# A Mamba-2 mixer: z of all four chunks at once, step widths one slot sooner, statistics of the first norm in other slots

## The reference, cut to what matters

```python
zxbcdt = x @ in_proj_w.T
z, xBC, dt = jnp.split(zxbcdt, [D_INNER, D_INNER + CONV_DIM], axis=-1)
dt = jax.nn.softplus(dt + dt_bias)
xBC = silu(causal_conv(xBC, conv_w) + conv_b)      # 4 taps, per channel
xs, Bm, Cm = jnp.split(xBC, [D_INNER, D_INNER + D_STATE], axis=-1)
dA = jnp.exp(dt * -jnp.exp(A_log))
# scan over tokens: h = h * dA_t + dt_t * x_t (outer) B_t;  y_t = h . C_t
y = (y + D * xs) * silu(z)
y = y * rsqrt(mean(y * y) + eps) * norm_w
return y @ out_proj_w.T
```

## Time and profile before

| what | value |
|---|---|
| median of 3 runs | 643.15 us (638.3 to 648.62) |
| profiled execution, time | 639.96 us |
| profiled execution, span | 638.0 us |
| mean granted TensorE clock | 0.929 |
| TensorE busy | 546.5 us, 86% |
| VectorE busy | 444.5 us, 70% |
| ScalarE busy | 360.4 us, 56% |
| GpSimd busy | 267.7 us, 42% |

### The profile page before, as it was taken

The page is one execution under the profiler, slowest core; times in us unless marked ns, Lnnn a source line. Parts: engine busy times, 40 slices in busy tenths (PEclk is TensorE's granted clock), DMA queues, the critical chain, the costliest instruction groups (busy, mean ns, idle before and its releaser), DMA issues.

```text
span 638.0 us, 13876 instructions
## 1 busy us (share of the span) xinstructions
PE 546.5 (86%) x3457; PEld 452.1 (71%) x3457; DVE 444.5 (70%) x1657; ACT 360.4 (56%) x1013; POOL 267.7 (42%) x324
## 2 busy tenths in 40 slices
PE   5588888898998989978789999973599999999593
PEld 3467677776777877766467877763599999999441
DVE  3746868577776657768568999997366666666267
ACT  4767584848485674834446656641266556666234
POOL 2213323241314123322102666677266666676333
PEclk9889999889998789989989999995699999999797
DMA  9399999990000000000064111111222222222383
GB/s 271 115 256 172 182 179 186 172 188 19 0 18 1 2 17 2 17 1 17 18 173 142 44 36 44 40 39 56 56 66 72 66 74 69 69 69 65 111 210 100
DMA packets 76395, 54.78 MB, mean 86 GB/s; under 512 B 10524, under 2 KB 69408, under 8 KB 76184
## 3 DMA queue, kind: packets, MB, share of 16 engines
q1 hardware_dynamic: 70352, 43.39, 33.9%
q0 software_dynamic: 4320, 8.99, 4.2%
q10 hardware_dynamic: 1640, 1.45, 0.7%
HBM read 40.62 MB, written 31.58 MB: 113 GB/s over the span
## 4 chain that ended last, share of the span: by engine, by line
PE 40%; issue 34%; DVE 11%; POOL 10%; DMA 4%; ACT 1%; ACTq 1%; POOLq 0%; SPq 0%; DVEq 0%
PE bank L1852 11%; PE bank L1870 10%; PE bank L1722 3%; PE bank L1738 3%; POOL arena L279 2%; PE bank L1728 2%; POOL arena L291 1%; POOL queue L1277 1%; DMA arena<-in_conv_w 1%; PE bank L1843 1%; POOL arena L267 1%; POOL x L297 1%; PE bank L1713 1%; POOL arena L294 1%; DVE nmx L1485 1%
## 5 line engine op out<-in xcount | busy, mean ns | idle before, releaser
L284 POOL TENSOR_TENSOR arena<-arena,half_neg 128x1 f32<-128x1 f32 x32 | 17.6, 550 | 196.0 <-ACT arena L442 196.0
L1317 POOL DMA_INDIRECT results<-arena x71 | 75.7, 1067 | 55.0 <-ACT arena L1416 50.4
L1852 PE MATMUL bank<-front,arena 128*128 128x128 f32 x568 | 78.5, 282 | 1.1 <-issue 0.3
L1870 PE MATMUL bank<-h_all,front 128*128 x568 | 75.5, 276 | 0.1
L1277 POOL DMA_INDIRECT queue<-arena,pos x64 | 63.1, 985 | 28.5 <-issue 13.8
L1852 PEld LDWEIGHTS bank<-front,arena 128*128 128x128 f32 x568 | 70.6, 195 | 4.3 <-issue 3.1
L1870 PEld LDWEIGHTS bank<-h_all,front 128*128 128x128 f32 x568 | 69.4, 193 | 0.3 <-issue 0.3
L1635 DVE COPY arena<-arena 128x516 f32 x71 | 35.9, 506 | 42.5 <-PE bank L1852 34.6
L684 PE MATMUL bank<-h_hi,wc_hi 128*128 128x512 f32 x96 | 46.6, 486 | 15.5 <-ACT arena L436 15.5
L1410 ACT ACTIVATE front<-bank 128x128 f32<-128x128 f32 x71 | 19.7, 278 | 53.6 <-PE bank L1843 52.7
L1648 DVE TENSOR_SCALAR front<-bank,arena 128x128 f32<-128x128 f32 x142 | 42.8, 342 | 4.7 <-PE bank L1852 4.5
(11 more groups left out here) (282 smaller groups left out, 1498.1 us busy)
## 6 DMA issues: line engine op xcount, KB each, us to landing
queue<-in_pad_rows SPq DMA_DIRECT2D x8, 2178.0 KB, 33.1
arena<-queue SPq DMA_DIRECT2D x71, 66.0 KB, 1.9
rows<-mod_rows SPq DMA_DIRECT2D x8, 384.0 KB, 6.3
x_keep<-x SPq DMA_DIRECT2D x8, 256.0 KB, 2.3
arena<-in_w SPq DMA_DIRECT2D x1, 2048.0 KB, 8.8
h_all<-in_w SPq DMA_DIRECT2D x1, 2048.0 KB, 8.6
h_all<-results SPq DMA_DIRECT2D x8, 256.0 KB, 4.8
arena<-results SPq DMA_DIRECT2D x8, 256.0 KB, 5.1
```

The source lines that it names most:

```text
L1317: pool.indirect_dma_start(k.results, bass.IndirectOffsetOnAxis(ap=xg[:, c, D:D + 1].bitcast(I32), axis=0), yw[:, c, :], None).then_inc(S[f ...
L1852: mm = t_.matmul(bank[(2 if g < NG // 2 else 6) + p][:, g * P:g * P + P], wc[:, p, g * P:g * P + P], xt[:, p, :], start=True, stop=True)
L1870: mm = t_.matmul(bank[4 + p][:, 0:D], ht[:, p, g * P:g * P + P], w2[:, e, g, :], start=(g == 0), stop=(g == NG - 1))
```

## The change

Four things.

1. TensorE computes all four z products of a slot c = 0 ahead of the chunk's product (L791 to L799), where two stood behind it. ScalarE evicts all four at the head of the slot.
2. silu(z) of the last chunk of a sequence gets three buffers instead of two, so that its eviction waits for the gating product of f - 3. The arena grows by 256 columns.
3. The step widths move from slot c = 1 into c = 0: DVE's first two operations behind L551, ScalarE's exp and ln behind its four copies and ahead of L414 and the flat eviction, DVE's last two into the end of the slot. ScalarE's exp(dt * A) and the silu table load move to the head of slot c = 1.
4. The first norm's statistics, for sequences 3 to 7, are taken in slots c = 0 (chunks 0 and 1) and c = 1 (chunks 2 and 3) instead of four in slot c = 2. In slot c = 0 they stand behind L593 and ahead of L607. The addition L639 moves with them to c = 1. POOL's root L304 stays in c = 2, L521 and L450 in c = 3.

```diff
-        zs = sb("zs", [P, 2, NC, DI]); xn1 = ...
+        zs = sb("zs", [P, 2, NC - 1, DI]); zs_last = sb("zs_last", [P, 3, DI]); xn1 = ...
+        def z_rows(f, i):
+            return zs[:, f % 2, i, :] if i + 1 < NC else zs_last[:, f % 3, :]
 # ScalarE, z_leaves
-                if f >= 2:
-                    wait(act, "s_yz", NC * (f - 2) + i + 1)
+                ago = 2 if i + 1 < NC else 3
+                if f >= ago:
+                    wait(act, "s_yz", NC * (f - ago) + i + 1)
 # ScalarE, body, head of the slot
                 if front and c == 0:
-                    z_leaves(f, 0)
-                    z_leaves(f, 1)
-                if front and c == 1:
-                    ... (wait d_neg; exp; wait d_exp; ln)
+                    for i in range(NC):
+                        z_leaves(f, i)
 ...
+                if front and c == 1:
+                    ... (wait d_dax; exp into da48; early silu)
 # ScalarE, body, behind the copies
                 if front and c == 0:
-                    z_leaves(f, 2)
-                    z_leaves(f, 3)
+                    ... (wait d_neg; exp; wait d_exp; ln)
                 ... (L414)
-                if front and c == 1:
-                    ... (wait d_dax; exp into da48; early silu)
                 if front and c == 0:
                     flat_leaves(f)
 # VectorE, body, behind L551
+                if front and c == 0:
+                    ... (L526, L537, which stood before and behind L534 for c == 1)
 ...
-                if gl < NB and c == 2:
+                norm = ({2: (0, 1, 2, 3)} if gl < 3 else {0: (0, 1), 1: (2, 3)}).get(c, ()) if gl < NB else ()
+                if norm:
                     wait(dve, "l1_ag", NC * gl)
-                    for i in range(NC):
+                    for i in norm:
                         v.bn_stats(st1[:, i, :], x[:, gl * NC + i, :]).then_inc(S["l1_st"], 1)
                 if chunk(s) and c == 0:
                     ... (L607)
 ...
-                if gl < NB and c == 2:
+                if norm and norm[-1] == NC - 1:
                     ... (L639)
-                if front and c == 1:
+                if front and c == 0:
                     ... (L643), and the same for L651
 # TensorE, body
                 if front and c == 0:
-                    z(f, 0)
-                    z(f, 1)
+                    for i in range(NC):
+                        z(f, i)
 ... (L791 to L799 of chunk s - 1)
-                    if front and c == 0:
-                        z(f, 2)
-                        z(f, 3)
```

More of the change, by code:

```diff
@@ L383, in body @@
                                   bias=mod[:, 0, 0, g:g + 1]).then_inc(S["f_ev"], 1)
+                if front and c == 1:
+                    wait(act, "d_dax", f + 1)
+                    act.wait_ge(S["set_pool"], 1)
+                    if f >= 1:
+                        wait(act, "o_w", seventh["da", f - 1] + 1)
+                    ac.activation(da48[:].rearrange("p (i w) -> p i w", i=3)[:, 0::2, :], dax[:].rearrange("p (o w) -> p o w", o=1).broadcast_to([P, 2, NC * NH]),
+                                  ACT.Exp).then_inc(S["d_da"], 1)
+                    ac.activation(early[:], ones[:, 0:1], ACT.Silu)
                 if between:
@@ L407, in body @@
                 if front and c == 0:
-                    z_leaves(f, 2)
-                    z_leaves(f, 3)
+                    if f == 0:
+                        act.wait_ge(S["w_in2"], 16 * 6)
+                        ac.activation(a_exp[:], a_log[:], ACT.Exp)
+                    wait(act, "d_neg", f + 1)
+                    ac.activation(dte[:], dtn[:], ACT.Exp).then_inc(S["d_exp"], 1)
+                    wait(act, "d_exp", f + 1)
+                    ac.activation(dtl[:], dte[:], ACT.Ln, bias=1.0).then_inc(S["d_ln"], 1)
                 if chunk(s) and c < 3:
@@ L552, in body @@
                                     bank[2][:, DI:DI + P].rearrange("p (o i) -> p o i", o=1).broadcast_to([P, NH, P]), ALU.mult).then_inc(S["s_mt"], 1)
+                if front and c == 0:
+                    wait(dve, "f_ev", ring["z", f, 3] + 1)
+                    wait(dve, "d_dt", f)
+                    v.tensor_tensor(dtw[:].rearrange("p (k h) -> p k h", h=NH), dtr[:].rearrange("p (k h) -> p k h", h=NH),
+                                    dt_b[:].rearrange("p (o h) -> p o h", o=1).broadcast_to([P, NC, NH]), ALU.add).then_inc(S["d_raw"], 1)
+                if front and c == 0:
+                    wait(dve, "d_raw", f + 1)
+                    v.scalar_tensor_tensor(out=dtn[:], in0=dtw[:], scalar=-1.0, in1=dtw[:], op0=ALU.mult, op1=ALU.min).then_inc(S["d_neg"], 1)
                 if front and c == 3:
@@ L626, in body @@
                         dve.nop(nofuse=True).then_inc(S["o_r"], 1)
-                if gl < NB and c == 2:
-                    wait(dve, "l1_st", NC * (gl + 1))
-                    for i in range(NC):
+                if norm:
+                    wait(dve, "l1_st", NC * gl + norm[-1] + 1)
+                    for i in norm:
                         v.bn_aggr(mv1[:, i, :], st1[:, i, :]).then_inc(S["l1_ag"], 1)
@@ L809, in body @@
                         t_.matmul(bank[4][:, 0:DI], b_rows[:, t % 2, :], xdw[:, t % 2, :], start=True, stop=True).then_inc(S["s_smm"], 1)
-                elif front and c == 0:
-                    z(f, 2)
-                    z(f, 3)
                 if front and c == 0:
@@ L1076, in after_mixer @@
             late[0] += n
-            assert late[0] <= 19568
+            assert late[0] <= 19824
             return k.carve(late[0] - n, shape)
```

27 lines of the change are left out of this document (6 added, 21 removed).

## The result

| what | before | after |
|---|---|---|
| median, first comparison | 644.9 us (638.3 to 648.6) | 655.9 us (654.2 to 659.2) |
| ratio to before, 95% interval | | 1.021 (1.015 to 1.027) |
| median, second comparison | 652.1 us | 661.1 us |
| ratio to before, 95% interval | | 1.015 (1.008 to 1.022) |
| profiled execution, time / span | 639.96 / 638.0 us | 659.21 / 657.2 us |

What follows compares the result with a forecast made beforehand. It took the mixer for a TensorE stream whose few stalls are paid in full, with half clock on top. -8.9 + 11.1 - 0.4 + 1.5 = +3.3 us on 639.96 gave 643.3, by the median 646.5; forecast 645, range 638 to 652.

Steps and rivals of the forecast that it cites:

- The trade: TensorE's 1.78 us stall in slots c = 2 goes, about 2.5 us at the out-projection of c = 0 comes; chance 0.55.
- c = 2, stall at the convolution gone: ScalarE no longer idles 1.78 us, so TensorE's wait for L436 goes in five slots c = 2: -8.9 us.
- c = 0, out-projection later: L607 and the out-projection come 2.03 us later in four slots, 1.60 and 1.4 in two: +11.1 us.
- c = 3: Slots c = 3 stay near 8.0 us, as L521 still waits for POOL's L304: -0.4 us over four.
- clock: New stall brings half clock in five of six slots c = 0 and 1; 7.4 + 5.6 against 11.5: +1.5 us.
- The stall for z(2)'s bank: In slot c = 0 TensorE waits 0.55 us until ScalarE has evicted z(0), whose bank z(2) writes.
- the two long slots: Two slots c = 0 with two smaller stalls each, at half clock before; their 5.6 us was taken to stay.
- Rival B: Slower: clock stays low for longer, six slots c = 0 pay 2.8 us each; +12.7, 653 to 656 us; chance 0.2.
- Rival A: Faster: the new stall at the out-projection does not come, L607 having slack; -15.2, 625 to 628 us; chance 0.13.
- Rival C: ScalarE is not freed, its exp waiting for DVE's negated widths; +8, 648 to 651 us; chance 0.1.
- The term for c = 0: Two of the four statistics in DVE's run before L607 delay the out-projection by 0.43 us in four sequences.
- a cover of 5 us: If POOL's L291 holds the moved L639 in c = 1, about 5 us of DVE idle before L548 hides it.

Runs made afterwards that it cites:

- The second pair: Kernel after and kernel before profiled once more without an edit; after 661.11 us for 652.1 before, ratio 1.015.
- e9_filler: Kernel after plus four extra matmuls on TensorE, result unread, in each slot c = 0 inside the stall before the sums' copy; 650.2 us, ratio to before 1.005.
- e6_both: Kernel after with the sums copied directly behind the scan and ScalarE's copies of c = 1 ahead of its exp; 624.16 us, ratio to before 0.983.
- e10_all_waits: Kernel after with sums early, ScalarE's copies first, statistics in c = 2, z(2) and z(3) behind the product; 635.7 us, ratio to before 0.979.
- e3_third_buffer: Kernel before with only the third buffer for silu(z) of the last chunk; 630.47 us, ratio to before 0.995.
- e5_copies_first: Kernel after with ScalarE's exp and silu load of c = 1 back behind the slot's copies and scaled rows; 650.24 us in a single execution.
- e2_stats_back: Kernel after with the first norm's statistics back in slot c = 2; ratio to before 1.013.
- e1_sums_early: Kernel after with DVE's copy of the cumulative sums directly behind the scan of slot c = 0; ratio to before 1.017.
- both experiments on it: Kernel after with statistics back in c = 2, ratio to before 1.013; kernel before with only the statistics moved, 644.3 us median for 638.8.

## Why the prediction was wrong

**The account.** The two first profiles differ by 19.2 us. The mixer has 7.2 of it, the slots from 27 to the start of attention 1.5 (46.0 for 44.5 us), what lies ahead of slot 3 0.2, attention 8.4 and the rest 1.9. The second pair gives 6.0 and 1.4 for the first two. So 7.4 to 8.7 us repeat and lie where the code was changed. The medians differ by 9 to 11; the remaining 1 to 3 us lie in unchanged code and I can't tell them from its own variation. The second comparison is the cleaner one, as the attention stretch has its long form on both sides: 9.0 us between the medians, 8.2 between the profiles. The slots from 27 on had no term in my sum, though they are changed code. There too the clock is lower (0.61 and 0.73 in slots 29 and 30, 0.79 and 1.00 before); what else is in their 1.5 us I haven't taken apart.

**The trade, term by term.** At full clock a sequence takes 8.19 + 7.08 + 9.57 + 8.07 = 32.91 us before and 10.26 + 6.77 + 7.50 + 8.38 = 32.91 after (c = 1 from `e9_filler`, the only run where it is at full clock with all of the change). Over slots 3 to 26:

| term | predicted | measured |
|---|---|---|
| c = 2, stall at the convolution gone | -8.9 | -10.3 |
| c = 0, out-projection later | +11.1 | +10.9 |
| c = 1 | 0 | -1.1 |
| c = 3 | -0.4 | +1.5 |
| clock | +1.5 | +6.1 |
| sum | +3.3 | +7.1 |

The traded stalls came as forecast: the stall of 1.78 us went, one of 2.30 came at the out-projection (about 2.5 forecast), slots c = 0 last 10.26 us (about 10.2). The stall for z(2)'s bank was 0.38 us for 0.55. But the first stall didn't go by ScalarE's relief alone. Counted from the start of slot c = 0 at full clock, the eviction ends at 17.79 us for 19.09 before, 1.3 us sooner (17.6 forecast), and TensorE comes to it at 18.87 for 17.11, 1.76 later. Had TensorE come as before, about 0.7 us would be left. `e6_both` (0.97 us) and `e10_all_waits` (1.45) show this: where TensorE is early again, the stall is back. That ScalarE's two idles add up to just 1.78 us was chance; `e3_third_buffer` took 1.42 of them away and 0.30 went from the stall.

Slots c = 2 went to 7.50, not 7.8, since a stall costs more than its idle time. In TensorE's timeline of a slot c = 2, before and after:

```profile
190.25 0.60 PE L765 MATMUL bank<-ident,arena 128*128 128x128 f32 x4
...
163.14 0.60 PE L768 MATMUL bank<-ident,arena 128*128 128x128 f32 x4
163.49 0.47 PE L687 MATMUL bank<-h_hi,wc_hi 128*128 128x512 f32 x1
```

After, the convolution's first matmul begins 0.35 us after the start of the transposes, while they still run; before, it begins 2.37 us after it (192.62 in the earlier trace rows), of which 1.78 is idle, so the overlap of about 0.25 us is lost too. The slots bear it out: 9.57, 9.25 and 8.74 us with stalls of 1.78, 1.48 and 0.97 are all 0.27 to 0.29 longer than 7.50 and their stall.

**The step that failed is the clock.** It said that the new stall brings half clock in five of six sequences at 1.5 us each, 7.4 us, beside 5.6 for the two long slots. The 1.5 us was taken from slots c = 2, where the lower clock lasts for part of a slot. The runs show 1.0 to 2.8 us each in its place. With the full-clock lengths of `e9_filler`, slots c = 1 of the kernel after are longer by 2.8, 2.2, 1.4, 2.2, 1.0 and 1.9 us: six of six, 11.5 us; the two long slots c = 0 by 3.2 and 2.2 (5.4, as forecast), the others by 0.9. That is 17.8 us for 11.7 before, +6.1. Of the 3.8 us by which the mixer missed my sum the clock has 4.6 and slots c = 3 have 1.9; slots c = 1 and 2 gave 2.5 back. `e9_filler` shows the cause: fill the stall and the mixer is 11 us shorter. What the sum missed is that the two traded stalls are not worth the same in the clock. Before, the 1.78 us was followed by half clock in four of six cases; the new ones of 2.30 and 1.91 us in every one, with smaller stalls of 0.43 and 0.38 us in the same slot.

Counted over all the profiles, half clock followed stalls in slots c = 2 as follows: of 0.94 to 1.19 us in none of 8 cases, of 1.43 to 1.48 us in 1 of 15, of 1.67 to 1.79 us in 15 of 20. The stalls of 1.90 to 2.30 us at the out-projection of c = 0 had it in 23 of 24 cases (the kernel after twice, `e5_copies_first`, `e2_stats_back`), those of 2.0 us at the out-projection of c = 1 in `e1_sums_early` in 3 of 6. So the length counts, and it isn't the length alone; what else does, no run separates.

**Rival B**, the clock low for longer, was the case that came; its sign, a mean clock under 0.92 over the mixer, is there (0.90). Its price, +12.7 us, was too high for the mixer (+7.2), since only two slots c = 0 paid about the 2.8 us (3.2 and 2.2). It had 0.2; the forecast had 0.55. Its 653 to 656 us met the median of 655.9, in part by chance, as the rest was added by unchanged code. That my sum started from one profiled execution of 639.96 us left out that the attention stretch alone moves such an execution by 9 us. The chance of 0.13 for slower by over 2% stood against what came out just at that border.

**Rival A** is excluded: L610 has no slack. **Rival C** too: exp waits 0.18 us for the negated widths, and ScalarE waits 0.84 us for TensorE where it was late before. The table load is followed by its exp without a drain again.

**Statistics.** The term for c = 0 was right in size (0.40 for 0.43) but not on the path: c = 1 gave it back, as both experiments on it show. The step for c = 3 (-0.4 us) failed in sign. It asked which instruction L304 waits for and took POOL's product ahead of it as fixed at 1.09 us; with L639 away DVE's L663 comes first, and the product takes 0.45 us more. L639 itself, for which I named a cover of 5 us, needed none (0.15 us).

**What the prediction did not see** is the second chain. It lists exp, silu and the copies of c = 1 in ScalarE's walk, and only asks whether L436 is in time. The copies, which the out-projection of c = 1 needs, went 2.9 us back in ScalarE's order by this move. In the kernel after the stall of c = 0 hides it. It changes nothing in the sum, but everything in what a repair would bring: with the sums alone moved, nothing is gained.

## What to carry to other kernels

When a stall goes because another is put in its place, compare what follows them in the clock, not only their lengths: here two orders with the same 32.9 us per sequence at full clock differed by 6 us. When an edit moves work ahead of several consumers on one engine, walk every one of them, also those a larger stall hides; removing one of two parallel chains shows nothing, and only the pair tells. When a wait disappears, ask whether the one waited for came sooner or the one waiting came later: the second is no gain. And take a second profile of the kernel before, before a sum is set against the first.

## What the runs showed of the hardware

- Useless matmuls can pay: 1.9 us of them per sequence in a stall of 2.3 us took 27 us of half clock and 10.9 us of the mixer's time away.
- TensorE stalls of 1.4 to 1.5 us in slots c = 2 were followed by half clock in 1 of 15 cases, of 1.7 to 1.8 us in 15 of 20.
- A TensorE stall in front of a matmul cost its idle time and 0.27 us of lost overlap with the matmuls ahead of it.
- The order in which DVE and POOL come to two instructions of 128x512 decides which is stretched: POOL's product 1.09 us with DVE's small one at 0.90, or 1.54 us beside DVE's 0.69.
- The clock's pattern in the mixer repeated to 0.1 us in two executions of the kernel after, while that of the kernel before changed slots. A stretch of unchanged code further on took 142.2 to 144.2 us in nine profiles and 150.6 to 152.3 in five. The kernel before has one of each, with every engine's busy time within 2 us of the other's.
